# Second attention, sums of exponentials: four TensorE products into the bank of scores, and a shorter sum on VectorE

## The reference, cut to what matters

```python
def _L0_attn_b_ref(x, Wq, Wk, Wv, Wo, bo):
    ...
    q = (x @ Wq.T).reshape(N, S, H, hd).transpose(0, 2, 1, 3)
    ...
    att = jnp.einsum('nqhd,nkhd->nhqk', q, k)
    att = jax.nn.softmax(att / jnp.sqrt(jnp.asarray(hd, x.dtype)), axis=3)
    out = jnp.einsum('nhqk,nkhd->nqhd', att, v).reshape(N, S, D)
    return out @ Wo.T + bo
```

## Time and profile before

| what | value |
|---|---|
| median of 3 executions | 871.89 us |
| the profiled execution, its own time | 874.01 us |
| its span in the trace | 871.8 us |
| PE busy | 774.4 us, 89% |
| weight loads (PEld) busy | 597.6 us |
| DVE busy | 651.1 us, 75% |
| ACT busy | 482.0 us, 55% |
| POOL busy | 418.2 us, 48% |
| mean granted clock of PE | 0.965 of full |

### The profile page before, as it was taken

One profiled execution on the slowest core, in us unless ns is written; L12 is line 12 of the kernel. 1 busy time (PEld: TensorE's weight loads), 2 busy tenths in 40 slices (PEclk: granted clock), 3 DMA queues, 4 the chain that ended last, 5 costly groups with the idle time before them and its releaser, 6 DMA issues.

```text
span 871.8 us, 25743 instructions
## 1 busy us (share of the span) xinstructions
PE 774.4 (89%) x10372; PEld 597.6 (69%) x10372; DVE 651.1 (75%) x1528; ACT 482.0 (55%) x853; POOL 418.2 (48%) x326
## 2 busy tenths in 40 slices
PE   0899999999999999999999996968899999859695
PEld 0688888888888888888888855555466555535554
DVE  3676677677667767676677796556999999998654
ACT  1586767767766876686668543323444444315341
POOL 1344444445444534454444620014998888893000
PEclk9999999999999999999999996999999999977699
DMA  7000000000000000000000000000111222221002
GB/s 296 2 3 2 0 0 0 0 0 0 0 0 0 0 0 0 0 0 0 0 0 2 3 0 1 1 2 1 20 22 22 24 24 24 25 25 13 1 1 97
DMA packets 71589, 13.26 MB, mean 15 GB/s; under 512 B 66432, under 2 KB 70528, under 8 KB 70912
## 3 DMA queue, kind: packets, MB, share of 16 engines
q1 hardware_dynamic: 71552, 12.76, 6.7%
HBM read 8.56 MB, written 4.19 MB: 15 GB/s over the span
## 4 chain that ended last, share of the span: by engine, by line
PE 67%; DVE 13%; ACT 7%; issue 6%; POOL 4%; DMA 3%; DVEq 0%; SPq 0%; ACTq 0%; POOLq 0%
PE PS L568 6%; PE PS L525 6%; PE PS L357 6%; PE PS L358 4%; PE PS L359 4%; PE PS L437 4%; POOL b_w L941 3%; PE PS L561 3%; PE PS L778 3%; PE PS L547 2%; DVE b_prod L893 2%; PE PS L768 2%; DVE a_nm L651 2%; PE PS L532 2%; ACT a_ph L597 2%
## 5 line engine op out<-in xcount | busy, mean ns | idle before, releaser
L684 POOL TENSOR_TENSOR a_pl<-a_p,a_ph 128x1024 f16<-128x1024 f32 (+1 forms) x128 | 210.4, 1644 | 256.8 <-ACT a_ph L597 256.8
L941 POOL TENSOR_TENSOR b_w<-b_v,b_e 128x2048 f32<-128x2048 f32 x32 | 137.8, 4308 | 11.6 <-ACT b_e L859 11.6
L594 ACT ACTIVATE a_p<-PS 128x1024 f32<-128x1024 f32 (+1 forms) x128 | 103.7, 810 | 70.9 <-PE PS L532 70.9
L651 DVE TENSOR_REDUCE a_nm<-PS 128x4 bf16<-128x512 f32 (+1 forms) x128 | 121.5, 949 | 0.0
L587 ACT ACTIVATE a_qk_h<-PS 128x512 f16<-128x512 f32 x128 | 73.3, 603 | 58.3 <-PE PS L359 57.0
L597 ACT ACTIVATE a_ph<-PS 128x1024 f16<-128x1024 f32 (+1 forms) x128 | 103.0, 805 | 0.0
L640 DVE TENSOR_TENSOR a_qk_l<-PS,a_qk_h 128x512 f16<-128x512 f32 x128 | 87.0, 681 | 3.4 <-ACT a_qk_h L587 3.4
L893 DVE TENSOR_TENSOR b_prod<-PS,b_qt 128x512 f32<-128x512 f32 x128 | 80.4, 678 | 9.0 <-PE PS L770 8.2
L380 POOL TENSOR_TENSOR veps<-mv,eps 128x2 f32<-128x2 f32 (+1 forms) x52 | 11.2, 215 | 146.1 <-DVE mv L1250 119.5
L357 PE MATMUL PS<-xhl,a_wqk_h 128*128 128x256 f16 x256 | 71.4, 279 | 8.3 <-ACT xhl L585 7.5
L547 PEld LDWEIGHTS PS<-a_vh,a_ph 128*128 128x128 f16 x768 | 69.5, 97 | 10.8 <-issue 9.2
(11 more groups left out here) (232 smaller groups left out, 2020.9 us busy)
## 6 DMA issues: line engine op xcount, KB each, us to landing
scratch_dram<-b_o SPq DMA_DIRECT2D x32, 64.0 KB, 4.1
b_y<-scratch_dram SPq DMA_DIRECT2D x16, 128.0 KB, 2.1
out_dram<-X SPq DMA_DIRECT2D x2, 1024.0 KB, 3.9
w_rest<-rest_dram SPq DMA_DIRECT2D x1, 1862.0 KB, 15.2
X<-x_dram SPq DMA_DIRECT2D x1, 1792.0 KB, 11.2
w_first<-first_dram SPq DMA_DIRECT2D x1, 1600.0 KB, 7.0
w_rolls<-rolls_dram SPq DMA_DIRECT2D x1, 544.0 KB, 15.7
X<-x_dram SPq DMA_DIRECT2D x1, 256.0 KB, 3.8
```

Source lines behind the costliest of these rows:

```text
L594: act.activation((a_p0, a_p1)[j][:, me, :, :, :].rearrange("p a h q -> p a (h q)"), TT[:, :, 0:512 - 256 * j], ACT.Exp, scale=EA ** -0.5)
L651: dve.tensor_reduce(a_nm[:, nx, j, :].rearrange("p (a h) -> p a h", a=2)[:, :, 0:2], MM[:, :, 0:256 * (j + 1)].rearrange("p a (h k) -> p a ...
L684: pool.tensor_tensor(*(n[:, g % 2, :, :, :].rearrange("p a h q -> p (a h q)") for n in (pl, p, ph)), ALU.subtract).then_inc(a_split, 1)
L941: pool.tensor_tensor(b_w8[:, j, :, :, :], rolled_values(par, j, 0, H), rolled_exps(par, j, 0, H), ALU.mult).then_inc(b_weighed, 1)
```

## The change

A new step "partial" stands behind "roll" 3, and "roll" 4 comes after it. In it PE makes four products of the unit matrix with a quarter of the exponentials each (for each of the 32 rows four neighbours out of 16, 128 columns), and adds them up in the first 128 columns of the bank that held the batch's scores. "sumexp" on DVE then sums four columns out of PSUM in place of sixteen out of SBUF, and waits for the four products instead of for the exponentials. "flip" 0, which overwrites the bank, waits for the reciprocal of the batch that used it last.

```diff
@@ b_steps
-    put(one, ("roll", 3), ("roll", 4))
+    put(one, ("roll", 3))
+    put(True, "partial")
+    put(one, ("roll", 4))
     put(True, "sumexp")
@@ b_tensor
+                elif kind == "partial":
+                    pe.wait_ge(b_exped, b + 1)
+                    for n in range(4):
+                        ins = pe.matmul(O[par][:, 0:128].rearrange("p (a s) -> p a s", s=4), ident[:, :],
+                                        b_e[:, par, :, :, 4 * n:4 * n + 4].rearrange("p t h s -> p (t h) s"),
+                                        start=n == 0, stop=n == 3, skip_group_check=True)
+                    ins.then_inc(b_partial, 1)
...
                     if j == 0:
-                        wait(pe, b_exped, b)
+                        wait(pe, b_divided, b)
@@ b_vector
                 elif kind == "sumexp":
-                    dve.wait_ge(b_exped, b + 1)
-                    link(dve.tensor_reduce(b_rs[:, par, :, :], b_e[:, par, :, :, :],
-                                           X_AXIS, ALU.add))
+                    dve.wait_ge(b_partial, b + 1)
+                    link(dve.tensor_reduce(b_rs[:, par, :, :].rearrange("p t h -> p (t h)"),
+                                           O[par][:, 0:128].rearrange("p (a s) -> p a s", s=4), X_AXIS, ALU.add))
```

More of the change, by code:

```diff
@@ L697, in build @@
         b_gathered, b_summed, b_divided = sem("b_gathered"), sem("b_summed"), sem("b_divided")
+        b_partial = sem("b_partial")
         b_stored, b_loaded, b_turned, b_added = sem("b_stored"), sem("b_loaded"), sem("b_turned"), sem("b_added")
```

## The result

The changed kernel takes **880.23 us** (median of 879.63, 880.23 and 880.70) against 871.89 before: ratio 1.0099, 95% interval 1.008 to 1.0118, so 7.0 to 10.3 us slower. The forecast was 878.4, range 874.7 to 883. The two profiled executions differ by less than the medians, 880.70 against 874.01 and 6.7 us in the span, since the one before was 2.1 us above its median.

A forecast was written before the change was run, and what follows sets the result against it. PE's way from roll 3 to roll 7 was taken to release DVE; 14 steps x 0.46 = 6.4, plus 0.1 for step 14 and 0 for step 15, gave +6.5 on 871.89: 878.4 us, range 874.7 to 883.

The forecast's parts named there:

- The bound: Second attention: PE releases DVE's rolls 6 and 7, so the shorter sum is worth 0 in steps 0 to 13.
- The sum: DVE's sum of four columns from PSUM takes 0.26 to 0.28 us, 0.40 us less than before, without a PSUM surcharge.
- The products and the slack: PE between rolls 3 and 4: products take 1.0 us, slack hides 0.54, dots 0 comes 0.46 us later per step.
- Steps 0 and 14: Second attention: step 0 loses 0.46 us like steps 1 to 13; step 14, without xt and xlow, loses 0.1.
- 0.4 at roll 4: Step 14: DVE loses 0.4 us waiting for PE's roll 4, and gains 0.40 at the sum.
- Step 15: Products behind yt: the sum starts 2.85 us late, DVE's stream is 2.45 late, cost to the whole time 0.
- The half clock that I priced: Step 15: PE at clock 0.50 after its DMA wait, so the products take some 2.0 us.
- The cover: After step 15: slack before the applies and b_y are used, and DVE's 2.54 us idle, just absorb the 2.45 delay.
- the rival with the uncovered tail: Step 15's delay is not absorbed, otherwise as forecast: +9.0 us in all, 880.9 us; chance 15%.

The follow-up runs named there:

- e1: Kernel before with DVE's sum cut from 16 exponentials to 4, read from SBUF, and no products on PE: 870.96 us, ratio 0.9987.
- e2: Changed kernel with the products kept on PE, but DVE sums 16 exponentials from SBUF without waiting for them: 879.67 us, ratio 1.0092.
- e4: Kernel before with xt and xlow moved behind roll 7 and DVE's sum cut to 4 exponentials, no products: 865.80 us, ratio 0.9928.
- e8: Like e6, but step 15's four products stand behind yt instead of ahead of it: 865.96 us, ratio 0.9933 to the kernel before.
- e9: Like e6, but with the four products in one block behind roll 3: 869.77 us, ratio 0.9981 to the kernel before.
- e6: Changed kernel with one product behind each of rolls 3 to 6, roll 7 before dots 0, xt and xlow later: 866.07 us, ratio 0.9938 to before.

## Why the prediction was right

**The bound.** Right, and the most important step. PE releases rolls 6 and 7; DVE is full because it is fed just in time. e1 (gain 0 per batch), e2 (the sum's length without effect) and e4 (gain as soon as the way is shorter) show it from three sides.

**The sum.** 0.26 to 0.28 us forecast, 0.281 on average from PSUM. The surcharge for a source in PSUM in the table under the TRN2 errata of "VectorE: DVE Perf Modes" (the Trainium skill) would have made it 0.34; the same sum of four from SBUF in e1 takes 0.276. The trace does not agree with it for this operation.

**The products and the slack.** Forecast 1.0 less 0.54 = 0.46 us per step; measured 0.44, but so close by luck, since two misses cancel. The products took 0.90, with nothing exposed for the first weight load; and the slack was 0.46, not 0.54: from roll 3's end to dots 0 PE needed 0.90 + 0.88 + 0.08 (698.59 to 700.45), and the last 0.08, ahead of dots 0's own first load, I had counted as slack. The grouped operand cost nothing: 0.11 per matmul, in agreement with the rule on cachelines that the forecast drew from "SBUF — State Buffer" (the Trainium skill).

**Steps 0 and 14.** Counted with 0.46 and 0.1; they lost 0.76 and 0.59. Timeline of step 14 in the changed kernel:

```profile
771.84 0.69 DVE L903 TENSOR_TENSOR b_prod<-PS,b_qt 128x512 f32<-128x512 f32 x1 [0.64 <-PE PS L773]
...
773.82 1.29 DVE L903 TENSOR_TENSOR b_prod<-PS,b_qt 128x512 f32<-128x512 f32 x2 [0.16 <-PE PS L773]
```

In the kernel before, DVE hardly holds PE back at rolls 4 and 5 in these two steps, so that there is almost no slack. In step 14 DVE now waited 0.64 us for roll 4 and 0.16 for roll 6, each with the lost overlap on top, and gained 0.40 at the sum. The forecast had taken its "0.4 at roll 4" from a step that has the slack. Steps 1 to 13 lost 5.94 together, 0.457 each. In sum 0.76 + 5.94 + 0.59 = 7.29 against 6.5. These two steps are 0.8 of the 1.8 us by which the forecast was short (878.4 against 880.23). The other 1.0 is not in this stage: the profiles show 0.6 us less outside it, and the medians are of three executions each, which lie up to 2.8 us apart.

**Step 15.** Timeline of the changed kernel, PE and DVE, and windows before and at the products:

```profile
781.45 0.41 PE L805 MATMUL PS<-w_first,b_y 128*128 128x128 f32 x2 [2.65 <-DMA b_y<-scratch_dram]
781.70 1.06 PE L779 MATMUL PS<-b_e,w_first 128*128 128x128 f32 x8
...
782.79 0.29 DVE L912 TENSOR_REDUCE b_rs<-PS 128x32 f32<-128x128 f32 x1 [2.69 <-PE PS L779]
...
793.98 2.05 PE L997 MATMUL PS<-w_first,f_xs 128*128 128x128 f32 x8
...
803.79 0.87 DVE L374 BATCH_NORM_STATS2 stats<-X 128x6 f32<-128x128 f32 x4 [0.28 <-ACT X L876]
```

```profile
779.00:781.40 2.40, 0.00 (x0) 0.00 (x0) 1.10 (x1) 0.27 (x1) 2.33 (x1) 1.00 0.18 55
781.40:782.60 1.20, 1.15 (x10) 1.14 (x10) 0.00 (x0) 0.38 (x1) 1.20 (x1) 1.00 0.00 0
```

The sum starts 4.40 us behind the last exponential's start (782.79 - 778.39) instead of 2.10 (773.47 - 771.37): 2.30 late, where 2.85 was forecast. The half clock that I priced was not there: PE's clock was still granted in full after 2.65 us without work, and the products took 0.9. In its place the DMA came later: PE's wait for it ended 3.06 us behind the last exponential's start (781.45 - 778.39) instead of 2.24 (773.61 - 771.37). The cover held as forecast: DVE's idle time before the last statistics shrank from 2.54 to 0.28 us, PE's use of the applies came 15.59 us behind the exponential (793.98 - 778.39), not later than 16.02 before, and the stretch behind the last exponential became no longer. So the rival with the uncovered tail is out, though the median of 880.23 lies nearer to its 880.9 than to 878.4. That the cover held is in part luck: only 0.28 us of it was left at full clock, and in e8's profile, with the late DMA and half the clock together, the same statistics came later.

## What to carry to other kernels

An engine that is busy 99% of a stage need not be its bound: look whether its instructions start just behind the end of another engine's, and follow the releaser's own order back to where it last waited. Work cut from the full engine is worth nothing unless it lies on that way, and work added to the other costs only what exceeds its waits, at the place where it stands. Here the same four products cost 0.45 us more as one block than spread over four waits (e9, e6), and the same shorter sum was worth 0 or 0.23 us by the order of two other steps (e1, e4).

## What was not expected

PE's clock after a pause differed between executions. Windows (columns as in rows 1), the kernel before, then the changed kernel:

```profile
773.10:773.30 0.20, 0.00 (x0) 0.00 (x0) 0.20 (x1) 0.00 (x0) 0.20 (x1) 0.96 0.02 3
```

```profile
783.20:783.50 0.30, 0.30 (x3) 0.30 (x3) 0.30 (x2) 0.00 (x0) 0.30 (x2) 0.70 0.00 0
```

At step 15 it was granted in full through 2.4 us without work and through the products in the changed kernel, and fell to half at about 783.3 us, while PE was busy. In the kernel before it fell within such a pause, at about 773.3 us, 1.5 us after PE's last matmul had ended, and was at half in the 2 us behind the pause.

And what lies ahead of the second attention, which is the same work in all of these kernels, ends earlier or later by some microseconds: its first exponential started between 595.1 and 601.3 us in the eleven profiles. The first attention accounts for the smaller part: ACT's last copy in it (a_ot) started between 501.8 and 504.1 us. The larger part comes between the two, where the granted clock differed: from 580 to 590 us it was 0.78 in the profile before and 1.00 in e6's. That is why periods tell these versions apart better than single times do.
